# One attention and expert layer on one core: where finished rows are gated, when GpSimd scatters them, and where the shared expert's pieces stand

## The reference, cut to what matters

```python
x = x + _L0_attn_ref(_layernorm(x), w_attn, w_proj, embk, embv)
x = x + _L0_ffn_ref(_layernorm(x), gate_w, gate_bias, w1, w3, w2, sw1, sw3, sw2)
# in _L0_ffn_ref, xt the 4096 rows:
scores = softmax(xt @ gate_w.T)
_, idx = top_k(scores + gate_bias, 2)
weights = take_along_axis(scores, idx, axis=1)
for e in range(8):
    gate_e = sum(where(idx == e, weights, 0.0), axis=1)
    h = silu(xt @ w1[e].T) * (xt @ w3[e].T)
    y = y + gate_e[:, None] * (h @ w2[e].T)
z = silu(xt @ sw1.T) * (xt @ sw3.T) @ sw2.T
return y + z
```

## Time and profile before

| | |
|---|---|
| three runs, us | 793.71, 793.95, 795.59 (median 793.95) |
| the profiled execution, us | 794.27 |
| its span in the trace, us | 792.5, so 1.77 lie around it |
| busy share of the span | PE 80%, PEld 62%, DVE 69%, ACT 60%, POOL 59% |
| granted TensorE clock, mean | 0.929 |
| end of GpSimd's last near_probs | 590.0 us |
| GpSimd's first and last scatter of a routed product | 606.9 to 758.1 us |
| last instruction | 792.5 us |

### The profile page before, as it was taken

The page is one execution under the profiler, slowest core; times in us unless marked ns, Lnnn a source line. Parts: engine busy times, 40 slices in busy tenths (PEclk is TensorE's granted clock), DMA queues, the critical chain, the costliest instruction groups (busy, mean ns, idle before and its releaser), DMA issues. The chain is left out here.

```text
span 792.5 us, 27444 instructions
## 1 busy us (share of the span) xinstructions
PE 634.0 (80%) x10064; PEld 488.2 (62%) x10116; DVE 545.0 (69%) x1840; ACT 473.2 (60%) x1006; POOL 466.4 (59%) x536
## 2 busy tenths in 40 slices
PE   4687788998879988977998796987748776756877
PEld 3465566776657776755677674666537664535744
DVE  7966676887778898877789776799635355323545
ACT  3686777878778877886777786666623232112211
POOL 9453355656366654886555788458662756774620
PEclk9879999999999999998999998999979778788899
DMA  9899989789888777896677779645622322325375
GB/s 259 260 290 321 346 278 288 208 253 275 275 246 248 221 208 213 260 261 210 214 212 239 213 215 267 183 155 188 208 63 79 91 71 74 95 69 163 83 224 147
DMA packets 150228, 161.91 MB, mean 204 GB/s; under 512 B 13676, under 2 KB 115825, under 8 KB 149776
## 3 DMA queue, kind: packets, MB, share of 16 engines
q1 hardware_dynamic: 145488, 151.67, 64.5%
q0 software_dynamic: 4608, 8.47, 3.2%
HBM read 93.87 MB, written 67.26 MB: 203 GB/s over the span
## 5 line engine op out<-in xcount | busy, mean ns | idle before, releaser
L1116 ACT ACTIVATE work<-ps,nmin 128x128 f32<-128x128 f32 (+3 forms) x512 | 248.1, 546 | 94.6 <-DVE nmin L1207 81.9
L1207 DVE CUSTOM_DVE_ANT_0 ps<-ps,near 128x128 f32<-128x128 f32 (+3 forms) x512 | 244.4, 508 | 80.2 <-PE ps L941 58.0
L953 PE MATMUL ps<-ident,work 128*128 128x128 f32 x1280 | 207.6, 283 | 50.0 <-issue 33.4
L953 PEld LDWEIGHTS ps<-ident,work 128*128 128x128 f32 x1280 | 159.9, 146 | 69.3 <-issue 38.2
L892 POOL TENSOR_SCALAR_AFFINE_SELECT work<-work 128x512 f32<-128x512 f32 x96 | 61.5, 640 | 152.2 <-ACT work L1105 117.6
L1192 DVE COPY work<-ps 128x512 f32<-128x512 f32 (+1 forms) x192 | 123.0, 641 | 31.8 <-POOL work L888 14.7
L896 POOL TENSOR_TENSOR work<-work 128x512 f32<-128x512 f32 x96 | 124.5, 1296 | 8.0
L941 PE MATMUL ps<-kb,qb 128*128 128x384 bf16 (+3 forms) x460 | 112.4, 303 | 11.8 <-ACT work L1116 9.0
L1599 POOL DMA_INDIRECT parts<-near,vb x80 | 78.4, 979 | 59.8 <-DVE near L1924 38.6
L1105 ACT ACTIVATE work<-ps 128x512 f32<-128x512 f32 (+1 forms) x160 | 89.9, 562 | 25.7 <-PE ps L953 14.4
L970 PE MATMUL ps<-work,vb 128*9 128x128 f32 x2560 | 97.3, 280 | 2.4 <-issue 1.2
(11 more groups left out here) (172 smaller groups left out, 873.9 us busy)
## 6 DMA issues: line engine op xcount, KB each, us to landing
near<-w_slots SPq DMA_DIRECT2D x96, 512.0 KB
w_slots<-relS SPq DMA_DIRECT2D x128, 256.0 KB, 4.9
qk_rows<-work SPq DMA_DIRECT2D x36, 256.0 KB, 5.1
near<-w_slots SPq DMA_DIRECT2D x32, 256.0 KB
vb<-slots SPq DMA_DIRECT2D x80, 65.0 KB, 1.9
qb<-parts SPq DMA_DIRECT2D x16, 256.0 KB, 4.2
qk_rows<-y SPq DMA_DIRECT2D x9, 256.0 KB, 6.6
qb<-qk_rows SPq DMA_DIRECT2D x24, 96.0 KB
```

Source lines behind the costliest of these rows:

```text
L953: ins = nc.tensor.transpose(tp_ps[:, m % 2, n * P:(n + 1) * P], prob[:, m % PROBS, n * P:(n + 1) * P], ident[:, :])
L1116: ins = nc.scalar.activation(prob[:, m % PROBS, h * wide:(h + 1) * wide], qk_ps[:, m % 3, h * wide:(h + 1) * wide], ACT.Exp, bias=nmin[:, ...
L1207: nc.vector.tensor_tensor_reduce(out=scores, in0=scores, in1=near[:, q % NEAR, a, 4 * P - wide:4 * P, r], scale=1.0, scalar=3e38, op0=ALU. ...
```

## The change

- The turned rows of stage e - 1 ride in the bank of yb(e), beside its own turned rows, and ScalarE copies both at once into one buffer of 512 columns (both). The gate scores and the ranks ride in pj(e); VectorE copies the scores out and reads the ranks straight from PSUM. Slots and banks of their own for stage 11 go away. RIDE_RK and the chain come at the same place in each group, in the slots behind pj(4g + 4) and pj(4g + 5).
- normalise() stands behind the last quad that ends at or before three slots after pj(e), so one quad earlier for most stages, and for stage 14 it now stands in attention, behind quad 126.
- GpSimd's scatters stand two to a quad, on quads of row blocks 2 and 3 that carry no normalise(). For group 0 these are quads 59, 60, 61, 63 to 67, for group 1 quads 91, 92, 93, 95 to 99, for group 2 quads 123, 124, 125 and 127; the last 8 of group 2 stand behind attention, ahead of normalise(15).
- The first map, the pads and the loads of the first tiles stand in the steps behind attention: the map in step 2, the pads in SyncE's step 3, the first tile loads in step 7, behind the store of stage 15's x1. In their place at the end of attention SyncE loads the first two chunks of turned rows.
- One list (ORDER) holds pairs and shared pieces, 64 steps: 8 shared pieces beside stage 15's pieces, 28 pairs of lot A with 12 shared pieces between them, 12 pairs of lot B, then 4 pieces. Tile buffers are 9; SyncE loads a pair 6 steps ahead.
- The shared product of a chunk is added to x1 at once and kept (sum_shared, into acc, for all 8 chunks). finish() adds the two routed parts; for chunks 0 to 5 it stands in steps among lot B's pairs, for chunks 6 and 7 behind all.

```diff
-NX = 8
+NX = 9
...
+def norm_quads():
+    return {e: max(q for q in range(NQ) if last(q) + 4 <= SLOT_OF["pj", e] + 3) for e in range(GI - 1)}
...
+        ready = SLOT_OF["pj", NI * g + NI + 1] + 3
+        free = [q for q in range(NQ) if last(q) + 4 >= ready and row(q) >= 2 and q not in NORM_AT.values()
+                and (row(q) == NI - 1 or q % QUADS < QUADS - 2)]
...
+                at[q] = (g, left[0], 2)
...
+                    if e:
+                        experts["turn"](pe, e - 1, bank[:, BESIDE:])
...
-                    nc.scalar.activation(ynT[:, :, :], misc("yb", e)[:, 0:GB * P].rearrange("p (b t) -> p b t", b=GB),
-                                         ACT.Copy).then_inc(ynT_done, 1)
+                    nc.scalar.activation(both[:, e % 2, 0:wide], misc("yb", e)[:, 0:wide], ACT.Copy).then_inc(ynT_done, 1)
...
+EARLY_STEPS = 8
+A_SHARED = 12
+B_SHARED = 1
+LEAD = 6
...
+    at = [shared.pop(0) for k in range(EARLY_STEPS)]
+    for lot, many in ((0, A_SHARED), (1, B_SHARED)):
+        for k in range(PAIRS[lot]):
+            at.append(lot * PAIRS[0] + k)
+            if (k + 1) * many // PAIRS[lot] > k * many // PAIRS[lot]:
+                at.append(shared.pop(0))
+    return at + shared
...
+TURN_STEP = 9
+CHAIN_STEPS = {11: range(0, 2), 13: range(2, 7), 14: range(7, 12), 15: range(12, 18), 16: range(18, 20), 17: range(20, CHAIN)}
+EXP_STEP = 12
+RANK_STEP = 16
+MAP_STEP = (2, 18)
+SPREAD_STEPS = {18 + k: k for k in range(TOPK * GB * NI)}
+LAST_A = max(step for step, j in PAIR_AT.items() if j < PAIRS[0])
+FINISH_AT = {LAST_A + 9 + c: c for c in range(GB * LOTS[0])}
+REST_AT = {LAST_A + (5 + c if c < 2 else 8 + c): c for c in range(GB * LOTS[0])}
+STORE_AT = {step + 1: c for step, c in FINISH_AT.items()}
...
+        for step in range(STEPS):
+            if step == 3:
+                store_pads(sp, 0)
+            if step == 6:
+                keep_turned(sp, EARLY + 2)
+            if step == 7:
                 store(GI - 1)
...
+            for at, j in PAIR_AT.items():
+                if step == max(at - LEAD, FIRST_PAIR - 1):
+                    load_pair(sp, j)
...
     def pool_program(pool):
+        for n in range(SPREAD_LEFT, TOPK * N8):
+            spread(pool, G - 2, n, 1)
+        normalise(pool, GI - 1)
         for step in range(STEPS):
...
+            if j == 0:
+                pe.wait_ge(shT_done, EARLY_HIDDEN)
+                pe.wait_ge(acc_done, EARLY_SUMS)
             pe.wait_ge(tile_in[j % NX], part_count(j))
...
+        def sum_shared(c):
+            dve.wait_ge(z_ready, c + 1)
+            dve.wait_ge(x1_in[c % 2], 16 * (c // 2 + 1))
+            nc.vector.tensor_tensor(acc[:, c, :, :], ps[:, sum_bank(c), :].rearrange("p (n c) -> p n c", c=C), x1c[:, c % 2, :, :],
+                                    ALU.add).then_inc(acc_done, 1)
```

More of the change, by code:

```diff
@@ L176, in schedule @@
     before.update({("yb", e): ("yt", e, 0), ("pj", e): ("yt", e, 1)})
[L177 to L183, removed]
+    bank.update({("xt", e): highest - 1, ("lg", e): highest - 1, ("rk", G - 1): highest - 1})
+    before.update({("xt", e): ("rv", e), ("lg", e): ("xt", e), ("rk", G - 1): ("lg", e)})
     return ops, bank, before, holder
@@ L1306 @@
[L1306 to L1319 removed]
+CHUNKS = TILES * P // CH
@@ new lines, with expert_steps @@
+EARLY_STEPS = 8
+A_SHARED = 12
+B_SHARED = 1
+LEAD = 6
+def expert_steps():
+    shared = []
+    for c in range(CHUNKS):
+        shared += [("hidden", c, 0), ("hidden", c, 1)] + ([("product", c - 1)] if c else [])
+    shared.append(("product", CHUNKS - 1))
+    at = [shared.pop(0) for k in range(EARLY_STEPS)]
[5 more added lines that the diff above has]
+    return at + shared
@@ new lines, with shared_banks @@
+ORDER = expert_steps()
+STEPS = len(ORDER)
+PAIR_AT = {step: item for step, item in enumerate(ORDER) if isinstance(item, int)}
+SHARED_AT = {step: item for step, item in enumerate(ORDER) if not isinstance(item, int)}
+FIRST_PAIR = min(PAIR_AT)
+LAST_PAIR = max(PAIR_AT) + 4
+EARLY_HIDDEN = sum(step < FIRST_PAIR and item[0] == "hidden" for step, item in SHARED_AT.items())
+EARLY_SUMS = sum(step < FIRST_PAIR and item[0] == "product" for step, item in SHARED_AT.items())
+def shared_banks():
+    banks = []
+    for step, item in SHARED_AT.items():
+        if item[0] == "hidden":
+            choice = ((1, 2), (3, 4)) if step < FIRST_PAIR else ((0, 7), (1, 2)) if step > LAST_PAIR else ((0, 7),)
+            banks.append(choice[len(banks) % len(choice)])
+    return banks
@@ L1320, in expert_part @@
+def expert_part(nc, ctx, t, ps, x1_done, ynT_done, lgr_done, chain, pj_ready, exp_done, x1_dram, xT_dram, slots, parts, gate_w, gate_bias, w123, out):
     CT = CH // P
@@ L1520, in sync_program @@
-        for c in range(CHUNKS):
-            if 2 < c + 2 < CHUNKS:
-                load_turned(sp, c + 2)
+            for at, j in PAIR_AT.items():
+                if step == max(at - LEAD, FIRST_PAIR - 1):
+                    load_pair(sp, j)
+            if step == MAP_STEP[1] + 2:
+                store_pads(sp, 1)
+            for at, (kind, *what) in SHARED_AT.items():
+                if step == at + 1 and what[0] + 2 < CHUNKS:
+                    if kind == "hidden" and what[1] == 1:
+                        load_turned(sp, what[0] + 2)
+                    if kind == "product":
+                        load_x1(sp, what[0] + 2, wait_stored)
@@ L1787, in hidden_banks, with sum_bank @@
     def hidden_banks(k):
-        return (0, 7) if sum(("hidden", *divmod(k, 2)) == piece and step <= LAST_PAIR for step, piece in SHARED_AT.items()) \
-            else ((0, 7), (1, 2))[k % 2]
+        return SHARED_BANKS[k]
+    def sum_bank(c):
+        return 5 if c < EARLY_SUMS else 6
     def same_before(k):
```

335 lines of the change are left out of this document (133 added, 202 removed).

## The result

The changed kernel takes 754.5 us (median of 4 runs, 752.3 to 757.5) against 794.8 of the kernel before beside it: ratio 0.949, 95% interval 0.945 to 0.954. The profiled execution took 755.63 us, its span is 753.8. Executions over 1.5% slower than the fastest of their kernel are left out of all times, ratios and stage lengths in this text, e5's and e6's profiled ones among them.

What follows compares the result with a forecast made beforehand. Attention was taken as a balance of VectorE, ScalarE and TensorE, the pairs as bound by GpSimd's scatters plus waits. The terms 585 + 36 + 134 + 14 gave 769 us in the trace, 771 in all; range 755 to 788.

Steps and rivals of the forecast that it cites:

- The last band: End of attention: GpSimd's last band ends at 585 us instead of 590, bounds 579 and 591.
- Attention before 534: Attention up to 534 us: a balance of VectorE, ScalarE and TensorE that the change hardly touches; no gain counted.
- Scatters moved within groups 0 and 1: GpSimd in attention: moved scatters stay under a quad's time and cost nothing, unless a quad is shorter than 4.5 us.
- the whole excess: End of attention, 534 to 590: all 7 us (55.8 - 48.7) over the same stage one group earlier go.
- choice between 585 and 591: End of attention: 585 if scatters get their turn beside the experts' weights, 591 if these hold one for 5.6 us again.
- The front: From the last band to the first product scatter: an in-order chain of 36 us instead of 16.9, bounds 32 and 42.
- The pairs: Routed pairs: 134 us, lot A 98 and lot B 36, nothing between the lots; bounds 125 and 147.
- The lower clock: Rival in the pairs: TensorE at 1.2 GHz throughout becomes the bound, 184 us replace 134, total 821; chance 0.05.
- The tail: After the last scatter: 14 us instead of 34.4, bounds 12 and 17, four shared pieces beside the last pairs' scatters.
- The front is shorter: Rival: band at 579, 32 us to the first product scatter, pairs 128, total 755; chance 0.15.
- SyncE's order in the pairs: Rival in lot A: SyncE waits for each of 12 pieces before loading on, 23 us, total 794, no change; chance 0.07.
- the rounds' waits: Rival in the pairs: rounds keep their waits, 147 us instead of 134, total 783; chance 0.18.

Runs made afterwards that it cites:

- e5: Changed kernel with 32 idle reductions put on VectorE in slots 303 to 318 (stages 13 and 14); 757.4 us, ratio 0.949 to the kernel before.
- e6: Changed kernel with 32 idle reductions put on VectorE in slots 322 to 337 (stage 15); 757.6 us, ratio 0.951 to the kernel before.
- e1: Changed kernel with normalise() of stages 3, 7 and 11 one quad later, at quads 39, 71 and 103; 762.9 us, ratio 0.958 to the kernel before.
- e3: Changed kernel with normalise() at quads 39, 71, 103 and scatters of groups 0 and 1 on quads 64 to 71 and 96 to 103; 770.0 us.
- e7: Kernel before with normalise() at quads 38, 70, 102 and scatters of groups 0 and 1 on their stages' first six quads; 793.3 us, ratio 0.998.
- e13: Kernel before with the gate's three own turns due 17 slots later, so they, ranking, map and group 2's scatters stand in stage 15; 795.7 us.
- e11: Changed kernel with the first map at step 0, normalise() of stage 14 behind the last band and no scatters on quad 126; 749.8 us.
- e8: Kernel before with group 2's scatters two a quad over quads 120 to 127 instead of four over 120 to 123; 800.1 us, ratio 1.006.
- e12: Changed kernel with lot A's 12 shared pieces in a row between the lots and lot B's one behind lot B; 783.0 us, ratio 0.987.
- e10: Changed kernel with the first lot's map at step 0 instead of step 2; 749.5 us, ratio 0.944 to the kernel before.
- e9: Kernel before with group 2's scatters two a quad over quads 120 to 127 and the first lot's pads stored from slot 346; 793.0 us.

## Why the prediction was wrong, point by point

**The last band, 585 forecast, 563.3 measured.** This is the step that failed, at three sentences of it. "Attention before 534 is a balance of VectorE, ScalarE and TensorE that the change hardly touches" gave 0; measured are -18.2 (534.2 to 516.0), of the 21.7 that the term was off; some 3 of them are this profile's own. "Scatters moved within groups 0 and 1 stay under a quad's time and cost nothing" weighed them against a quad of four units; the quads behind them are of one, and there normalise and scatters stood on the path: 8 to 11 us (e1 to e3), as long as a stage's sum on GpSimd fits (e7). The prediction's own condition, a quad shorter than 4.5 us, is the one that came: stage 13's quads take 1.4 us in the changed kernel (11.1 / 8). That the gate's own turns and the ranking of group 2 lay in stages 12 to 14 I counted with the copies alone, at 1 us; they held 6.7 (e13). The copies themselves did not lengthen the full-row stages, which run 47.5 us and not 48.8. Third, "the whole excess" of stage 15, 7 us: it was 4.3 us too small (stage 15 is 8.3 shorter with the 3.0 of normalise(14) in it, which e11 confirms, so 11.3), and its cause was read only half. Besides the four scatters a quad and the scatter that stood, SyncE's pads ahead of weights and relative scores were a second wait behind the first (e8), which I saw only as pads that leave the stretch.

On the weights, the changed kernel's trace shows two scatters at 541.60 and 543.03, both inside the transfer that was issued at 536.76 and took 8.6 us, with no idle time over 0.31 us ahead of them or of the third at 546.20. The Trainium skill (DMA: Bandwidth & Descriptors, Queues, rings and completion order), by which a scatter gets its turn beside the weights, agrees with that end. But the forecast's choice between 585 and 591 turned on the wrong thing. The scatter that stood in the kernel before is the 15th of its group's 16, and that one stands in the changed kernel too, 3.63 us, with the weights long landed. There it lies behind attention (577.15), 14.6 us ahead of the first tile load (591.71). The changed kernel is rid of the wait in stage 15 because that scatter moved. Two to a quad don't end it by themselves, as its groups 0 and 1 show (2.58 and 1.84 us), though in e8 none is left.

**The front, 36 forecast, 41.8 measured,** at its upper bound of 42. The chain is the one forecast, and the map took 5.3 us for 5.4. The sizes that were off are TensorE's: at clock 0.50 after each of two pauses, two early shared matmul groups took 2.08 and 1.91 us instead of 1.02, the product 3.62 instead of 1.95. And the four steps from the first turn of tiles to the first scatter took 10.9 us (594.21 to 605.06) for 8.4: a shared hidden piece of 1.9 us stands in them, which the sum left out, and TensorE waits 1.2 us for the second pair's tiles. "TensorE at its lower level at first" stood among the bounds.

**The pairs, 134 forecast, 136.6 measured,** lot A 99.0 for 98 and lot B 37.3 for 36. Groups by line of the changed kernel from 563.3 on (busy, mean ns; idle before, by releaser):

```profile
L1591 POOL DMA_INDIRECT parts<-near x80 | 79.1, 989 | 46.6 <-DVE near L1927 25.5 <-issue 21.1
...
L1810 PE MATMUL ps<-ident,near 128*128 128x128 f32 x80 | 16.2, 284 | 7.2 <-DMA near<-slots 4.4 <-ACT near L1889 2.8
```

GpSimd's waits for weighing fell from 38.6 to 25.5 us and TensorE's for tiles from 26.8 to 4.4. GpSimd's longest stretch of scatters without a wait runs from 626.48 to 714.4. The lower clock didn't come: 0.97 in lot A, where it was 0.82, and 0.89 in e12's lot A, which has no pieces to fill the tile waits. The Trainium skill (Perfetto Trace Analysis, Optimization Strategy) says that interleaving regimes with different most-contended engines may improve the time; e12, which sets the pieces apart (and moves finish() with them), is 28.5 us slower.

**The tail, 14 forecast, 12.1 measured.** Nothing of the shared expert stands in it.

**The rivals.** "The front is shorter" named 755, which is the time that came, but by a band at 579 and a front of 32; neither is so, and its reason, that the stage runs against no stall, bears on stage 15 alone. That the number fits is chance. SyncE's order in the pairs, the rounds' waits and the lower clock did not come, by the rows above. The forecast's 0.3% for what a measurement can tell was too small: the four runs of the changed kernel spread over 0.7%.

## What to carry to other kernels

On an in-order helper engine, weigh work that is moved against the shortest step that follows within its buffers' reach, not against the step that it stands on, and sum the engine's work over the stage ahead. When a wait is to go, look for what comes second behind it: of the two causes of stage 15's excess, taking one away gave 2.6 us and both 8. And ask whether the end follows the place that gets earlier: 7 to 8 us of attention were worth nothing in the kernel before, where the loads waited for something else, while the map's 5.3 us were worth 4 to 5 in the changed one, where all waits for it (with overlapping intervals).

## What the runs showed of the hardware that was not expected

TensorE's granted clock was 0.50 (1.2 GHz) behind two pauses of the front: after 4.01 us idle, the stretch 563.3 to 569.0 is at 0.50; after 3.59 us idle, 581.5 to 586.0 is at 0.50:

```profile
563.30:569.00 5.70, 5.54 (x132) 3.01 (x132) 0.00 (x0) 0.60 (x1) 4.32 (x6) 0.50 0.12 39
...
581.50:586.00 4.50, 4.50 (x24) 4.50 (x23) 0.62 (x1) 0.60 (x1) 0.00 (x0) 0.50 0.34 58
```

So a small chain on another engine costs TensorE's wait and then the slower work behind it: without the map's 5.3 us e10's front is 7.6 shorter than this one (41.8 to 34.2), and 5.7 shorter than the mean of the seven, which vary by 3.8.

A load of relative scores that SyncE issued 0.56 us behind the weights reached VectorE 10.6 us after its issue (570.03 to 580.61, e8), where the median of such loads is 5.2 us from issue to landing in the changed kernel. What cured it in e9 was not the order of these two: the load still stands behind the weights there (558.25 and 556.17), but it is asked for 11.8 us earlier, ahead of the pads, and VectorE doesn't wait for it. No run asks for it ahead of the weights.

GpSimd's scatters into slots stand at one place only. Among the first 48 (groups 0 to 2) of each profile, every idle time over 0.6 us that no other engine ended lies ahead of a group's 15th scatter. It is 5.59 us in group 2 of the kernel before; in the changed kernel it is 2.58 and 1.84 us in groups 0 and 1, and this in group 2:

```profile
577.15 0.98 POOL L1583 DMA_INDIRECT slots<-rows_a,place  x1 [3.63 <-issue]
```

In the eight profiles that have the landing of the 14th scatter on record and show such a wait, the 15th starts 0.67 us after that landing. In e8's group 2, where the 14th landed 2.4 us ahead of the 15th's start, no wait shows, nor in e3's groups 0 and 1, where a normalise stands between the two. In the kernel before, the last four scatters of group 2 are issued one after another with nothing asked for between them. What makes the 15th wait for the 14th, and none of the others, is not shown.
